# The queries' inverse norm as the scale of the exponentials, in place of a product with the rotated queries

## The reference

```python
qkv = x @ Wqkv                                   # 128 -> 3 * 1024
q, k, v = (sh(t) for t in jnp.split(qkv, 3, -1)) # 16 heads of 64
q = l2norm(q) * qs                               # t / max(|t|, 1e-12)
k = l2norm(k) * ksc
q = q * cos * scale + rotate_half(q) * sin * scale
k = k * cos * inv + rotate_half(k) * sin * inv
# windows of 32 queries, each on its own 32 keys and the 32 before
sim = jnp.einsum('bhwie,bhwje->bhwij', bq, bk2) * 8.0
sim = jnp.where(mask, -jnp.finfo(sim.dtype).max, sim)
attn = jax.nn.softmax(sim, -1)
out = jnp.einsum('bhwij,bhwje->bhwie', attn, bv2)
out = out.transpose(0, 2, 1, 3).reshape(b, n, INNER) @ Wo
```

## Time and profile before

| | |
|---|---|
| median of three runs | 4082.11 us |
| profiled execution | 4079.09 us, its span 4077.2 us |
| busy: PE, PEld, DVE, ACT, POOL | 3769.5, 3141.1, 3329.4, 3208.0, 3370.7 us |
| mean granted TensorE clock | 0.983 |
| chain that ended last | PE 62%, DVE 22%, issue 8%, ACT 4%, POOL 3% |
| maxima L1593, `prob` L1611 | 768 each, 423 and 424 ns |
| multiplies L1300 | 768, 1051 ns |
| exponentials L1116 | 3072, 293 ns, and as many reads of the sum |

### The profile page before, as it was taken

How to read it: one execution, slowest core, us unless ns; L and a number is a source line. 1 busy time by engine, 2 the same in 40 slices (tenths; PEclk the granted TensorE clock), 3 DMA queues, 4 the chain that set the end, 5 groups by cost and what they waited for, 6 DMA issues and landing times.

```text
span 4077.2 us, 163553 instructions
## 1 busy us (share of the span) xinstructions
PE 3769.5 (92%) x61792; PEld 3141.1 (77%) x61792; DVE 3329.4 (82%) x8896; ACT 3208.0 (79%) x11601; POOL 3370.7 (83%) x2461
## 2 busy tenths in 40 slices
PE   7998885999989999989999899999899998999997
PEld 5665664888877888868888778888688887788886
DVE  7998887888878888878888788888788887888885
ACT  6888995888866888848888668888488886688883
POOL 4554445999978999959999779999599997799992
PEclk9999997999999999999999999999999999999999
DMA  3000000111112111112111121111121111111111
GB/s 87 0 0 1 0 0 21 39 39 38 37 37 55 38 38 37 41 36 54 38 37 38 35 56 39 36 39 39 37 54 37 37 39 35 41 38 37 39 39 42
DMA packets 302004, 145.50 MB, mean 36 GB/s; under 512 B 83989, under 2 KB 293779, under 8 KB 301459
## 3 DMA queue, kind: packets, MB, share of 16 engines
q1 hardware_dynamic: 301458, 137.25, 13.9%
HBM read 21.85 MB, written 2.10 MB: 6 GB/s over the span
## 4 chain that ended last, share of the span: by engine, by line
PE 62%; DVE 22%; issue 8%; ACT 4%; POOL 3%; DVEq 1%; SPq 0%; DMA 0%; ACTq 0%; POOLq 0%
PE bank L737 18%; PE bank L848 7%; PE pair L828 7%; PE pair L776 7%; PE bank L730 6%; PE pair L769 5%; PE pair L911 4%; PE bank L797 3%; DVE top L1517 3%; DVE by_sin L1569 3%; DVE norm L1576 2%; DVE qk_parts L1492 2%; DVE top L1593 2%; PE bank L714 2%; DVE prob L1611 2%
## 5 line engine op out<-in xcount | busy, mean ns | idle before, releaser
L1288 POOL TENSOR_TENSOR rnorm<-norm2g,neg_half 128x16 f32<-128x16 f32 x384 | 1118.7, 2913 | 28.0 <-DVE norm2g L1586 22.7
L1280 POOL TENSOR_TENSOR rotated<-by_cos,by_sin 128x512 f32<-128x512 f32 x768 | 994.8, 1295 | 41.9 <-DVE by_sin L1569 41.6
L1116 ACT ACTIVATE pair<-pair,top 128x64 f32<-128x64 f32 x3072 | 895.0, 293 | 82.8 <-DVE top L1593 82.8
L1300 POOL TENSOR_TENSOR rotated<-rotated,rnorm 128x512 f32<-128x512 f32 x768 | 788.4, 1051 | 0.5
L737 PE MATMUL bank<-wqkv_high,xt_high 128*128 128x512 f32 (+1 forms) x1536 | 661.7, 431 | 13.2 <-ACT squares L1107 12.1
L1107 ACT ACTIVATE squares<-bank 128x512 f32<-128x512 f32 x768 | 458.7, 597 | 258.5 <-DVE by_sin L1569 217.3
L1116 ACT ACTIVATION_READ_ACCUMULATOR pair<-pair,top 128x1 f32 x3072 | 654.6, 213 | 0.0
L776 PE MATMUL pair<-qk_t 64*32 64x64 f32 (+1 forms) x18432 | 608.7, 217 | 0.0
L1561 DVE TENSOR_TENSOR by_cos<-bank,rot_cos 128x512 f32<-128x512 f32 x768 | 528.3, 688 | 82.7 <-PE bank L737 45.0
L1593 DVE TENSOR_REDUCE top<-pair 128x4 f32<-128x256 f32 x768 | 325.1, 423 | 279.3 <-PE pair L776 274.1
L1576 DVE TENSOR_REDUCE norm<-squares 128x8 f32<-128x512 f32 x768 | 519.2, 676 | 10.8 <-ACT squares L1107 10.1
(11 more groups left out here) (151 smaller groups left out, 8980.1 us busy)
## 6 DMA issues: line engine op xcount, KB each, us to landing
vmoved<-vout_all SPq DMA_DIRECT2D x1152, 64.0 KB, 2.1
ctx_all<-vout_all SPq DMA_DIRECT2D x384, 64.0 KB, 2.1
wqkv_sb<-in_L_ffn_Wqkv_dram SPq DMA_DIRECT2D x36, 256.0 KB, 3.8
ctx_all<-y SPq DMA_DIRECT2D x48, 128.0 KB
ctx_all<-y SPq DMA_DIRECT2D x48, 127.0 KB
wo_sb<-in_L_ffn_Wo_dram SPq DMA_DIRECT2D x6, 512.0 KB, 10.1
out_dram<-y SPq DMA_DIRECT2D x8, 256.0 KB, 3.5
w_sb<-in_L_ffn_W_dram SPq DMA_DIRECT2D x6, 341.0 KB, 3.3
```

Of the source, the lines that this page charges most:

```text
L1116: last = nc.scalar.activation(at, at, ACT.Exp, bias=top[jl % 2][:, h:h + 1], accum_out=psum_raw[jl % 2][:, h:h + 1])
L1280: nc.gpsimd.tensor_tensor(rotated[j % 4][:, :, :, :], by_cos[j % 2][:, :, :, :], by_sin[j % 2][:, :, :, :], ALU.add).then_inc(c_rot, 1)
L1288: nc.gpsimd.tensor_tensor(rnorm[slot][:, :, :].rearrange("t g n -> t (g n)"), norm2g[slot][:, :, :].rearrange("t g n -> t (g n)"), neg_hal ...
L1300: nc.gpsimd.tensor_tensor(at, at, rnorm[slot][:, i, :].unsqueeze(2).to_broadcast([P, 2 * HG, DH]), ALU.mult).then_inc(c_unit, 1)
```

## The change

The multiply of GpSimd now covers the keys alone (256 columns in place of 512). The inverse norm of the queries becomes the `scale` of the four exponentials, a pointer to one column of `rnorm`. Since the exponential's bias must then be the maximum times this norm, the vector engine writes the negated maxima to a new tile `peak`, and a new 128x4 product `top<-peak,rnorm` (`win_top`) stands right behind it; it waits for `c_peak`. `rnorm` has four buffers in place of two, because it is now read until the exponentials.

```diff
-        rnorm = ring("rnorm", 2, [P, 2, 2 * HG])
+        rnorm = ring("rnorm", 4, [P, 2, 2 * HG])
+        peak = ring("peak", 2, [P, HG])
...
-                        last = nc.scalar.activation(at, at, ACT.Exp, bias=top[jl % 2][:, h:h + 1], accum_out=psum_raw[jl % 2][:, h:h + 1])
+                        q = 2 * (h % 2) + h // 2
+                        last = nc.scalar.activation(at, at, ACT.Exp, bias=top[jl % 2][:, h:h + 1], scale=rnorm[jl // 2][:, jl % 2, q:q + 1],
+                                                    accum_out=psum_raw[jl % 2][:, h:h + 1])
...
-                    slot = j // 2 % 2
+                    slot = j // 2
...
-                    slot = (j // 2 - 1) % 2
+                    slot = (j // 2 - 1) % 4
...
-                        at = rotated[(j - 2) % 4 + i][:, :, :, :].rearrange("t a h d -> t (a h) d")
-                        nc.gpsimd.tensor_tensor(at, at, rnorm[slot][:, i, :].unsqueeze(2).to_broadcast([P, 2 * HG, DH]), ALU.mult).then_inc(c_unit, 1)
+                        at = rotated[(j - 2) % 4 + i][:, 1, :, :]
+                        nc.gpsimd.tensor_tensor(at, at, rnorm[slot][:, i, HG:2 * HG].unsqueeze(2).to_broadcast([P, HG, DH]), ALU.mult).then_inc(c_unit, 1)
...
-                    nc.vector.tensor_reduce(top[slot][:, :].rearrange("q (e i) -> q e i", e=2), win_ps[slot].rearrange("q e (i k) -> q e i k", i=2),
-                                            AX_X, ALU.max, negate=True).then_inc(c_top, 1)
+                    nc.vector.tensor_reduce(peak[slot][:, :].rearrange("q (e i) -> q e i", e=2), win_ps[slot].rearrange("q e (i k) -> q e i k", i=2),
+                                            AX_X, ALU.max, negate=True).then_inc(c_peak, 1)
+
+            def win_top(layer, it, j):
+                if here(it, j, WIN.top):
+                    m = layer * GROUPS + it * STEPS + j - WIN.top
+                    jl = (j - WIN.top) % STEPS
+                    dve.wait_ge(c_peak, m + 1)
+                    nc.vector.tensor_tensor(top[jl % 2][:, :].rearrange("q (e i) -> q e i", e=2), peak[jl % 2][:, :].rearrange("q (e i) -> q e i", e=2),
+                                            rnorm[jl // 2][:, jl % 2, 0:HG].rearrange("q (i e) -> q e i", e=2), ALU.mult).then_inc(c_top, 1)
...
                 win_max(layer, it, j)
+                win_top(layer, it, j)
                 win_norms(layer, it, j)
```

More of the change, by code:

```diff
@@ L372, in build @@
         c_rn = sem("c_rnorm")
+        c_peak = sem("c_peak")
         c_rot = sem("c_rotated")
@@ L1286, in win_rnorm @@
                     pool.wait_ge(c_nrm2g, g + 2)
-                    slot = j // 2 % 2
-                    nc.gpsimd.tensor_tensor(rnorm[slot][:, :, :].rearrange("t g n -> t (g n)"), norm2g[slot][:, :, :].rearrange("t g n -> t (g n)"),
+                    slot = j // 2
+                    nc.gpsimd.tensor_tensor(rnorm[slot][:, :, :].rearrange("t g n -> t (g n)"), norm2g[slot % 2][:, :, :].rearrange("t g n -> t (g n)"),
                                             neg_half[:, :], ALU.pow).then_inc(c_rn, 1)
@@ L1693, in drain @@
                     win_max(layer, ENDED, j)
+                    win_top(layer, ENDED, j)
                     win_add(layer, ENDED, j)
```

## The result

The changed kernel takes 4225.83 us, the median of four runs (4225.04 to 4228.91), against 4082.61 for the kernel before (four runs). The ratio is 1.0354, with a 95% interval of 1.0336 to 1.0372. The profiled span is 4224.3 us against 4077.2, at a mean granted clock of 0.979 against 0.983. So the change costs 143 us, where 153 were forecast.

The account below looks back on a forecast made before the run. Bound: the vector chain and TensorE waiting for each other, every second chain deciding. Loop op and holds (21.2 us), straight part, last steps and layer end make 25.6 us a layer, 154 over six: 4235 us, range 4155 to 4285.

Parts of the forecast that it names:

- likeliest case: Whole kernel: longer vector chain plus `top` held by GpSimd, 4235 us, own range 4200 to 4270, chance 0.60.
- op, loop: Loop: `top` lengthens each vector chain by 0.22 us; four of eight decide, 0.88 us per iteration, 13 iterations a layer.
- holds, loop: Loop: GpSimd's add holds `top` once per eight-step iteration, 0.75 us net, 13 iterations a layer.
- straight part: A layer's 11 straight steps: five chains pay for the added op, 1.0 us a layer, no holds costed.
- late steps: Some ten last steps of a layer: five chains of about 0.45 us net, 2.2 us a layer.
- layer end: End of a layer: two groups of exponentials on the chain of waits, 2 x (0.20 + 0.40) = 1.2 us.
- The two legs: Loop: vector chain and TensorE wait for each other; every second chain sets TensorE's time, the one between has 0.07 us spare.
- The hold, place and price: Step behind the loop's branch: the add after GpSimd's power holds two-SBUF-input `top` about 1.05 us, net 0.75 per iteration.
- the y row: Earlier trace: a vector op with two SBUF inputs took its usual 0.68 us inside GpSimd's power, so powers do not hold.
- The last ten steps: Near a layer's end, without new input: `top` held 0.4 us every second step, 2.2 us a layer with the op.
- GpSimd's half: GpSimd's halved multiplies: about 0.6 us each, worth zero since nothing waits for them, but clearing the add before `top` comes.
- The pointer: Pointer scale: 0.10 us more per exponential, covered by ScalarE's waits inside the stage, paid only at a layer's end.

Follow-up runs that it names:

- experiment 2: Kernel before with only the dependent 128x4 product added (maxima to `peak` in PSUM, times a tile of ones): 4144.29 us, ratio 1.0158.
- experiment 1: Changed kernel with `peak` in PSUM beside the scores, so `top` reads only one SBUF tile: 4155.19 us, ratio 1.0184.
- experiment 4: Kernel before with GpSimd's multiply on the keys alone, queries left without their norm: 4078.45 us, ratio 0.9998.
- experiment 5: Changed kernel with GpSimd's multiply over all 512 columns again, queries normalised twice: 4424.37 us, ratio 1.0845.
- experiment 3: Kernel before with only a pointer to a column of ones as scale of the windowed exponentials: 4082.92 us, ratio 1.001.

## Why the prediction was right

The time (4225.8) lies in the likeliest case's own range of 4200 to 4270, and the mechanism was the one named. The runs split the loss, here 146 us from the kernel before of their own set: 64.6 us for the op (experiment 2), 11 for pointer scale and halved multiply on top of it (experiment 1 less 2), 70.6 for the holds. Term by term, per layer:

| term | predicted | measured |
|---|---|---|
| op, loop | 11.4 | 0.099 x 104 steps = 10.3 |
| holds, loop | 9.75 | (3.94 - 3.84) x 104 = 10.4 in five layers, 0 in the third |
| straight part | 1.0 | op 0.9, holds (3.70 - 3.58) x 11 = 1.3 |
| late steps | 2.2 | (3.72 - 3.58) x 9 = 1.3 |
| layer end | 1.2 | 91.3 - 89.1 = 2.2 on average |

The measured terms make 148 us over six layers, and the two profiled spans differ by 147.1.

- **The two legs.** Right. One chain in two decides (experiment 2), and the maxima's wait of 29.2 us did not hide the op: it fell to 23.3 in experiment 2, and the op cost 64.6 us all the same. The growth of a chain was 0.20, not 0.22, and `prob` stands 0.06 before the matmul.
- **The hold, place and price.** Right in place, and near in price: the step behind the loop's branch, held by the add behind the power, in 12 of 13 iterations in five layers, at 1.21 us on average. That costs 10.4 / 12 = 0.87 us per iteration with the second hold below; 0.75 was taken. The held `top` also keeps the exponentials waiting 0.5 to 0.6 us once an iteration, where I had taken their delay as covered. The held op ends 0.02 after the add, so the tail of 0.14 from the earlier trace rows was too long. In 300 cases `top` started inside a power that had more than 0.25 us left (0.74 at most), and took 0.166 at most: no power holds, as the y row said. The page "SBUF — State Buffer" of the Trainium skill does not part a power from an add; the measurement does.
- **Missed: a second hold in the iteration.** The step after the held one is long in 61 of 78 cases, 0.44 us on average (the row of 1536.67). That add waited for `by_sin` until 1535.84, which the first hold had made late. I had put this add ahead of `top`. Experiment 1, with no hold, shows the same place as I had it: the add waits 0.32 in place of 1.34, and `top` comes as it ends.

```profile
1514.98 1.28 POOL L1284 TENSOR_TENSOR rotated<-by_cos,by_sin 128x512 f32<-128x512 f32 x1 [0.32 <-DVE by_sin L1573]
```

```profile
1516.25 0.16 DVE L1605 TENSOR_TENSOR top<-pair,rnorm 128x4 f32<-128x4 f32 x1
```

One of the 61 stands in an iteration without a first hold, the second layer's first. In the straight part 18 of 66 are long too (0.67 us on average), which I had costed at nothing.
- **Missed: the third layer.** I held every layer to be alike. This one has no hold in its loop, 0.01 us ahead of the add. Two errors of opposite sign, so the loop's sum came out near, and that part of the agreement is luck: predicted 58 us of holds, measured five times 10.4, which is 52.
- **The last ten steps.** A long `top` takes 0.56 us there, so it is held 0.4, as forecast. But it is one step in three (18 of 54), not one in two, and the late steps cost 1.3 us a layer, not 2.2.
- **GpSimd's half.** Zero in the kernel before (experiment 4), and it clears the second add, without which the kernel would be at 4424 (experiment 5). The 0.6 us forecast for a multiply is 0.614.
- **The pointer.** 0.084 us per exponential, 0.10 forecast; ScalarE shows no new bound in the loop, where its waits for sines are 9.1 us in 300 (20.0 before). At the end of a layer the exponentials stand on the chain more often than I said. The chain of waits there, after, against the earlier trace rows:

```profile
3541.81 1.66 ACT pair L1119 x8
3543.79 1.23 PE bank L850 x4
3547.04 1.66 ACT pair L1119 x8
3549.02 1.22 PE bank L850 x4
3552.55 1.65 ACT pair L1119 x8
3556.81 1.66 ACT pair L1119 x8
```

Four groups of exponentials stand on it here (three in the second and fourth layer), not two: 4 x (1.66 - 1.29) = 1.5 us. Between experiments 2 and 1, whose loops have one and the same period, the layer end grows from 88.5 to 90.1 us on average, and this is where their 11 us lie. That the pointer is the whole cause isn't shown: alone, in experiment 3, it brings the layer end from 89.1 to 89.6 only. In four layers one `top` at the end also runs into GpSimd's split of the MLP's weights (1.10 us on average, 1.55 at most), which I had not looked at.

Still open: why the third layer falls into the other regime. All layers issue the same loop, but they enter it in different phase. The holds don't make that phase: in experiment 1, which has none, `top` stands in the third layer at the add's very start too, and 0.05 to 0.13 us inside it in the others. No run set the phase.

## What to carry to other kernels

A small operation put into a chain that two engines hand back and forth costs half of what it adds to the chain per step when every second chain decides: 0.20 us gave 0.10 a step in the loops and 64.6 us in all. Before placing a vector operation with two SBUF inputs beside a busy GpSimd, look in the timeline for what GpSimd runs at that moment, and where that is an add or a multiply, put one input in PSUM (70.6 us here). An engine that costs nothing today may be the next bound: the halved multiply was worth 0 in the kernel before and 64 us once the maxima were gone, so a piece of a losing change is worth trying again behind the next one; with bounded scores, dropping the maxima and keeping this change gave 3976.8 us.

## What was unexpected of the hardware

- A 128x4 operation, 0.16 us alone, can be stretched to 1.18 us by one GpSimd add, and a power of 2.9 us never did it.
- Whether the hold occurs turned on 0.05 us of phase (`top` 0.04 us inside the add was held, 0.01 us before it was not), and it came in 12 of a layer's 13 iterations, or in none: 3.94 against 3.83 us a step in one and the same program.
